# Moving the projections of three batches out of their own block and into the attention units

## The reference, cut to what matters

```python
x = x + tanh(g_ffn[0]) * L0_ffn(layernorm(x))          # experts; 4 result rows per token are summed
x = x + tanh(g_xattn[1]) * L1_xattn(layernorm(x), ctx)
# L1_xattn, 16 heads of 16: q = x @ Wq;  k, v = split(concat(ctx, x) @ Wkv)   (64 + 1024 keys)
# attn = softmax(causal(q @ k.T * 16**-0.5));  out = (attn @ v) @ Wout + bout
```

## Time and profile before

| what | value |
|---|---|
| runs | 1520.47, 1516.33, 1518.87 us; median 1518.87 us |
| the profiled execution | 1516.78 us, span 1514.7 us |
| busy over the span | PE 1098.5, DVE 1013.6, ACT 636.7, POOL 485.8 us |
| projection block | from 640.9 to 864.3 us of the span |
| attention block | from 864.3 to 1404.9 us |
| one unit in the steady part | 30.7 us |

### The profile page before, as it was taken

How to read it: one execution, slowest core, us unless ns; L and a number is a source line. 1 busy time by engine, 2 the same in 40 slices (tenths; PEclk the granted TensorE clock), 3 DMA queues, 4 the chain that set the end, 5 groups by cost and what they waited for, 6 DMA issues and landing times. The chain is left out here.

```text
span 1514.7 us, 23799 instructions
## 1 busy us (share of the span) xinstructions
PE 1098.5 (73%) x8155; PEld 563.8 (37%) x8155; DVE 1013.6 (67%) x1856; ACT 636.7 (42%) x1280; POOL 485.8 (32%) x539
## 2 busy tenths in 40 slices
PE   4799984342409999706556469999999999988757
PEld 2455553121206666403223213333333333331646
DVE  4989875454545666545554488888888888870675
ACT  1455653111103333202122117777777777775430
POOL 1334331767760000077886141111111111111110
PEclk8999997666659999957677759999999999996989
DMA  6010100222279999933676521111211121100003
GB/s 209 21 43 21 42 1 18 87 87 86 91 262 223 254 249 256 234 113 93 207 232 196 141 78 39 39 39 46 68 40 38 39 64 51 39 2 1 1 0 111
DMA packets 183649, 146.24 MB, mean 97 GB/s; under 512 B 102638, under 2 KB 160494, under 8 KB 183546
## 3 DMA queue, kind: packets, MB, share of 16 engines
q1 hardware_dynamic: 162570, 102.61, 25.8%
q0 software_dynamic: 12288, 33.57, 6.8%
q10 hardware_dynamic: 8688, 8.66, 1.8%
HBM read 53.11 MB, written 68.55 MB: 80 GB/s over the span
## 5 line engine op out<-in xcount | busy, mean ns | idle before, releaser
L1783 DVE TENSOR_REDUCE small<-ps 128x2 f32<-128x960 f32 (+6 forms) x384 | 378.7, 1040 | 53.9 <-PE ps L1839 51.6
L1762 ACT ACTIVATE region<-ps 128x512 f32<-128x512 f32 (+5 forms) x768 | 343.1, 533 | 107.3 <-PE ps L1853 106.5
L1733 POOL TENSOR_SCALAR_AFFINE_SELECT region<-region 128x512 f32<-128x512 f32 (+2 forms) x160 | 87.3, 546 | 423.6 <-ACT region L1762 423.6
L1853 PE MATMUL ps<-region 50*128 50x512 f16 (+5 forms) x896 | 198.3, 331 | 29.0 <-ACT region L1762 25.3
L1929 PE MATMUL ps<-region 128*32 128x512 f32 (+5 forms) x1792 | 191.7, 501 | 2.5 <-POOL region L1733 1.9
L860 POOL DMA_INDIRECT expert_rows<-region,small x128 | 131.3, 1026 | 64.0 <-issue 35.9
L1201 PE MATMUL ps<-region 128*128 128x384 f16 x696 | 124.0, 329 | 37.6 <-DMA region<-expert_rows 37.3
L1839 PE MATMUL ps<-region 48*128 48x480 f16 (+6 forms) x896 | 139.6, 333 | 15.1 <-DVE small L1783 15.1
L1366 POOL DMA_INDIRECT region<-result_rows,home x128 | 132.8, 1037 | 38.0 <-issue 36.3
L1853 PEld LDWEIGHTS ps<-region 50*128 50x128 f16 (+1 forms) x896 | 54.3, 95 | 211.1 <-ACT region L1762 197.0
L475 POOL TENSOR_TENSOR region<-region,small 128x1024 f32<-128x1024 f32 x32 | 60.9, 1915 | 117.2 <-DVE small L586 117.2
(11 more groups left out here) (237 smaller groups left out, 1730.3 us busy)
## 6 DMA issues: line engine op xcount, KB each, us to landing
result_rows<-region SPq DMA_DIRECT2D x58, 384.0 KB, 4.1
region<-v_parts SPq DMA_DIRECT2D x16, 576.0 KB, 3.8
v_parts<-region SPq DMA_DIRECT2D x14, 576.0 KB, 8.9
region<-k_parts SPq DMA_DIRECT2D x96, 68.0 KB, 2.2
region<-q_parts SPq DMA_DIRECT2D x96, 64.0 KB, 2.1
k_parts<-region SPq DMA_DIRECT2D x16, 272.0 KB, 5.4
x_sb<-in_x ACTq DMA_DIRECT2D x8, 512.0 KB, 9.6
region<-in_w13T SPq DMA_DIRECT2D x16, 256.0 KB, 3.0
```

Source lines behind the costliest of these rows:

```text
L1733: nc.gpsimd.affine_select(out=t, in_=t, compare_op=ALU.is_ge, fill=0.0, base=r0, pattern=[[0, G], [1, w]], channel_multiplier=-1).then_inc ...
L1762: nc.scalar.activation(dst, src, ACT.Exp, scale=SCALE).then_inc(s_exp, 1)
L1783: nc.vector.tensor_reduce(nmp[:, qt, :, p0:p0 + np_, place], s_pair(n + first)[:, :, 0:np_ * nk] .rearrange("p e (h k) -> p e h k", h=np_) ...
L1853: ins = nc.tensor.matmul(o, k_of(rr, tbuf)[:, pair, kt * P:kt * P + rows], q_of(rr, tbuf)[:, pair, q0:q0 + nq], start=True, stop=True)
```

## The change

In the projection block only the two chunks of batch 0 are projected; chunk 2 is also fetched, summed and normalised there, and half of chunk 3 is fetched. Everything else of chunks 2 to 7 becomes further words in the order of the units: `G` a fetch on POOL, `C` two additions on DVE (eight `C` to a chunk), `B`, `A`, `W`, `R` and `M` the steps of the normalisation, `X` the transposes, `Q`, `K`, `V` the products, and `x`, `q`, `k` the remainders on DVE. A product now fills a whole pair of banks and is read by one ACT and one DVE instruction of twice the width. It takes one of the two pairs of the scores and holds it until its remainder is taken (for values: until ACT has moved them). Chunk c's queries and keys come near the end of one unit, its values early in the next; the last 64 keys of a batch (`K.2`) come with the values. An entry of `BESIDE` names a value product `PV` and, between slashes, what is put behind that word, behind the next `T`, and behind the next score.

Unit 0's parts are copied inside SBUF (`load_first`, 24 DMAs) instead of being stored and loaded, while the stores of batch 0 (now in quarters) go on behind them. SP stores batches 1 to 3 within the attention, and a unit's loads wait for its batch's stores. The bias addition moves to units 11 and 12. Loops of DVE, POOL and SP over units are written out.

```diff
-        qp = view(region0, "qp", [P, 2 * PARTS, KH, L], F16)
+        yg = view(region0, "yg", [P, 4, FETCH, TOPK, D], F32)
+        def load_first(sp, done):
+            for dst, parts, slots in ((q_of, qp, Q_SLOTS), (k_of, kp, K_SLOTS)):
+                ...   # 2 halves x 3 slots x 2 pairs
+                            sp.dma_start(dst(r, 0)[:, p, :], parts[at_:at_ + DH, part, 0, :]).then_inc(done, 16)
             @block.sync        # projection block
-                for b in range(B):
-                    ...
+                sp.wait_ge(s_dve, moved(turn[0, "k10"]))
+                store_parts(sp, 0, slice(0, KH), slice(0, CH), slice(0, CH), s_pfirst)
+                sp.wait_ge(s_dve, moved(turn[1, "k02"]))
+                load_first(sp, s_unit0)
+                store_parts(sp, 0, slice(0, 1), slice(CH, L), slice(CH, KEYS), s_pfirst)
+                sp.wait_ge(s_dve, moved(turn[1, "k12"]))
+                store_parts(sp, 0, slice(1, KH), slice(CH, L), slice(CH, KEYS), s_pstored)
             @block.vector      # projection block
-                for c in range(2 * B):
-                    ...
+                combine(0, 0) ... normalised(1)
+                x_low(1)
+                low(1)
+                combine(2, 0)
+                combine(2, 1)
+                statistics(2)
+                normalised(2)
+        BESIDE = {
+            0: ("9 / / X2.0 X2.1 / x2.0", "10 / / Q2.0 Q2.1 C3.0 C3.1 C3.2 K2.0 K2.1 q2.0 C3.3 / ",
+                "11 / / G4.0 G4.1 / k2.0", ...),
+            1: ("0 / / G4.6 / ", "1 / / G4.7 / ", "3 / / V2.0 V2.1 / C3.4 C3.5", "4 / / / v2.0 C3.6 C3.7",
+                "5 / / G4.8 G4.9 / B3.0", "6 / / A3.0 G4.10 G4.11 / W3.0 R3.0", "7 / / G4.12 G4.13 / M3.0",
+                "8 / / G4.14 G4.15 / M3.1", "9 / / X3.0 X3.1 / x3.0",
+                "10 / / Q3.0 Q3.1 C4.0 C4.1 C4.2 K3.0 K3.1 q3.0 C4.3 / ", "11 / / / k3.0"),
+            2: ("3 / / K3.2 V3.0 V3.1 C4.4 k3.2 V3.2 v3.0 / C4.5", "4 / / / v3.2 C4.6 C4.7", "5 / / G5.0 / ",
+                "6 / / G5.1 / B4.0", "7 / / A4.0 G5.2 / W4.0", "8 / / G5.3 / R4.0", "9 / / / G5.4",
+                "10 / / / M4.0 G5.5", "11 / / G5.6 / M4.1", "12 / / / G5.7", "13 / / / G5.8"),
+            ...   # 3, 5, 7, 9 like 0; 4, 8 and 6, 10 like 1 and 2; 11, 12: two x four bias additions (Y)
+        def take(key, hold_):
+            free = [(slot + 1 + i) % FREE for i in range(FREE) if not held[(slot + 1 + i) % FREE]]
             @block.sync        # attention block
+                def load(v):
+                    sp.wait_ge(s_pstored, (v // NG + 1) * P_STORES + 1)
+                    load_parts(sp, v, v % NBUF, s_load[v % NBUF])
+                    sp.wait_ge(s_vstored, (v // NG + 1) * V_STORES + 1)
+                    load_values(v, v % NBUF)
+                def store(b):
+                    sp.wait_ge(s_sread, moved_at["K", 2 * b + 1, 2][1])
+                    store_parts(sp, b, slice(0, KH), slice(0, L), slice(0, KEYS), s_pstored)
+                    sp.wait_ge(s_vread, moved_at["V", 2 * b + 1, 2][1])
+                    for g in range(NG):
+                        store_values(sp, b, g)
+                for u in range(UNITS - 1):
+                    if u + 2 < UNITS:
+                        sp.wait_ge(s_pv, u * len(steps) + 2)
+                        load(u + 2)
+                    maxima(u, (u + 1) % NBUF)
+                    if u in (1, 5, 9):
+                        store(u // NG + 1)
             @block.tensor      # attention block
+                def next_parts(kind, c, i):
+                    ...
+                    if i % 2 == 0:
+                        wait_free(key)
+                        pe.wait_ge(s_sread, moved_at["X", c, 0][1])
```

More of the change, by code:

```diff
@@ L1527, in _ @@
                         ins.then_inc(s_full, 1)
-                    for n in VALUES[h]:
+                    for n in VALUES[c]:
                         t0, nt = VT[n]
@@ L1735, in _, with diagonal @@
-                units(pool, body)
+                def diagonal(u, k):
+                    hf, kt, q0, nq, on_diag = steps[k]
+                    if not on_diag:
+                        return
+                    last = max(i for i, (kk, _) in enumerate(t_list) if kk == k)
+                    pool.wait_ge(s_exp, u * N_T + T_FREE + 2 * (last + 1))
+                    rows = min(P, KEYS - kt * P)
+                    r0 = q0 - (kt * P - CTX)
+                    w = min(nq, P - r0)
+                    t = pT[0:rows, k % 2, :, 0:w]
+                    nc.gpsimd.affine_select(out=t, in_=t, compare_op=ALU.is_ge, fill=0.0, base=r0,
+                                            pattern=[[0, G], [1, w]], channel_multiplier=-1).then_inc(s_diag, 1)
@@ L1737, in _ @@
+                for u in range(-1, UNITS):
+                    for kind, *i in plans[u]:
+                        if kind == "PV":
+                            diagonal(u, i[0])
+                        elif kind == "G":
+                            fetch(*i)
+                        elif kind == "R":
+                            ln_pool(nc.gpsimd, i[0] - FIRST_C, s_var, s_rstd)
+                        elif kind == "Y":
+                            add_bias(i[0])
             @block.scalar
@@ new lines, in transposed_scores @@
+                def transposed_scores(of, i):
+                    tbuf = of % NBUF
+                    k, h0 = t_list[i]
+                    nq = steps[k][3]
+                    if of == 0 and i == 0:
+                        pe.wait_ge(s_ones, NBUF * 2 * 16)
+                    if i == 0:
+                        pe.wait_ge(s_mrow, (of + 1) * 32)
+                    for half in range(2):
+                        pe.wait_ge(s_exp, of * N_T + 2 * i + half + 1)
+                        if half == 0 and nq > CH // 2:
+                            product(tbuf, i, h0)
+                    if nq > CH // 2:
+                        product(tbuf, i, h0 + 1)
+                    else:
+                        for h in range(G):
+                            product(tbuf, i, h)
```

810 lines of the change are left out of this document (492 added, 318 removed), and 15 rows, old and new, of the table BESIDE.

## The result

| | before | after |
|---|---|---|
| median, timed side by side | 1519.31 us | 1551.51 us |
| ratio, with its 95% interval | | 1.0228 (1.0191 to 1.0266) |
| profiled execution, its span | 1516.78, 1514.7 us | 1551.13, 1549.2 us |
| last row sums of unit 15 (end of the attention's DVE work) | 1403.53 us | 1435.61 us |

The changed kernel is 2.3% slower; 1524 was forecast and the range ended at 1550. The attention does start much earlier, and the units pay more than that back. The first view is the timeline of the hand-over from the projection block: the stores of values that ACT issues, SP's copies of unit 0's parts and its sixteen quarter stores (start, length, instruction). The last row is DVE's first maximum of unit 0.

The account below looks back on a forecast made before the run. POOL's fetch queue was taken to bound the projection block, DVE's maxima and PE's hand-over the attention. Start -134.5, units' words +119.0, load wait +21.1 gave +5.6: 1524 us on the median, range 1488 to 1550.

Parts of the forecast that it names:

- The start: Hand-over from projection to attention: the attention starts at about 729.8 instead of 864.3, saving 134.5 us (bounds 123 to 138).
- 24 copies at 0.46 (2.76 / 6) are 11.0: SP's queue before the attention: unit 0's copies take 11.0 us, 0.46 each, beside 7.7 for sixteen quarter stores.
- margin of 1.7: At the attention's start: 1.7 us added for the barrier and the values that ACT stores at the same time.
- Queries and keys: Units 0, 1, 3, 5, 7, 9: X, Q, K and remainders cost 9.6 us per site, 57.6 for six.
- Units 4 and 8: Values 5.9 us per unit and normalisation 2.4, plus POOL's delays; 17.8 for the two units.
- so I add 1 us each: Units 2, 6, 10: 1 us each for PE's granted clock of 0.50 after idling at N0.
- The load wait: Units 2, 6, 10: PE waits at N0 for the values' load, 4.5, 4.5 and 9.1; 21.1 us with the clock.
- Rival (3): The chain of stores and loads takes about 35 us; N0 waits 12.5, 12.5 and 17: 1548 us, chance 0.23.
- Rival (1): Loads come in time in units 2, 6, 10, so nothing waits at N0: -15.5, 1503 us, chance 0.27.
- Rival (2): In the units DVE alone counts and PE's products hide below its words: -42, 1477 us, chance 0.12.
- POOL and the bias: Fetches and power between selects cost 4.3 in unit 1, bias additions 1.25 in units 11 and 12; 10.1 in all.
- Wrong "at its root": Signs against the forecast: no wait at N0, units 0 and 3 below 38 us, or an attention starting after 740.

Follow-up runs that it names:

- the three edits: Changed kernel with each batch's first unit stored first (batches 1 to 3), batch 0's quarter stores behind the barrier, POOL's fetches and powers behind the selects: 1514.33 us, 0.9966 of before.

## Why the prediction was wrong

The mechanism was right in the main: a saving at the attention's start, paid back in the units and in a wait for loads. Two terms failed: the price of the copies and stores at the start, and the lower clock behind the value products, which the sum left at nothing. The sum was short by 28.7 us on the profiled frame (34.35 for 5.6). Term by term:

| term of the sum | forecast | measured |
|---|---|---|
| attention's start | -134.5 | -119.7 |
| unit 0 | 9.6 | 11.8 |
| units 3, 5, 7, 9 | 39.3 | 38.1 |
| unit 1 | 23.2 | 24.3 |
| units 4 and 8 | 17.8 | 24.3 |
| units 2 and 6 with the load wait | 32.2 | 34.0 |
| unit 10 with the load wait | 15.5 | 14.9 |
| units 11 and 12 | 2.5 | 3.6 |
| units 13 to 15 | 0 | 1.0 |
| behind the attention | 0 | 2.4 |

(The forecast by units is the prediction's 119.0 + 21.1, laid out by the units that it names for each word. Behind the attention the work is the same; PE's mean granted clock there is 0.85 for 0.89, and no run looked further.)

**The start, 14.8 short.** The failing step is "24 copies at 0.46 (2.76 / 6) are 11.0". They took 20.8. The 0.46 was that of a load from DRAM, and of the cheaper of the two rows of loads in the earlier trace rows; a copy inside SBUF, which no row showed, takes 0.63 without the values' stores beside it and 0.87 with them. The 0.60 that I named as a bound is the mean of the two rows, and was near the 0.63; but for the likely value I took the lower row of another kind of transfer, and I gave the values that ACT stores only a share in a margin of 1.7. The 16 stores took 10.2 for 7.7 (0.63 each for 0.48). I had halved the price of a whole store; they have a quarter of its bytes (64 and 72 KB for 256 and 272) and still took two thirds of its time. The copies also began at 712.8 and not at 709.4, 3.4 later, and of the margin 1.0 was left over: 9.8 + 2.5 + 3.4 - 1.0 is the 14.8 but for rounding. The 3.4 I don't put to the change: POOL's first fetch of the block stands at 647.73 in the profile after, at 643.71 before, and between 641.9 and 647.1 in the experiments, which change nothing ahead of it.

**Queries and keys, right in size.** 9.6 per site was forecast; units 3, 5, 7 and 9 show 9.2 to 10.1. Unit 5 agrees part by part with the prediction's walk: the copy of `mT` comes 7.2 later (7.3 forecast), N0's maximum 0.7 more (0.6), the rest 1.4 more (1.7). The additions hide as it said. What it did not say is how little the products matter: with a third of them the chain shortens by 1.6, and the clock takes that back.

**Units 4 and 8, 6.5 short.** The failing step is the lower clock: the sum has it for the load wait alone ("so I add 1 us each") and leaves it at nothing behind the value products. Up to the maxima ahead of the last one the terms were right: in unit 4 DVE is through with them 7.9 us later than in the old unit, and the 5.9 for the values and 1.9 for the statistics come to 7.8. Then DVE waits for PE's last score and for `mT`:

```profile
1002.30 0.69 DVE L1965 TENSOR_REDUCE small<-ps 128x4 f32<-128x512 f32 x1 [2.34 <-PE ps L2090]
1006.46 0.68 DVE L1981 COPY small<-ps 8x1024 f16<-8x1024 f16 x1 [2.74 <-PE ps L2153]
```

In the earlier trace rows these waits are 0.20 and 1.28, so 3.6 us are added, where the sum has 0.6 for POOL; in unit 8, which has no fetches, they are 1.87 and 2.74. The value products leave PE busy 6.4 of 10 us, the clock stays at the lower level for 13.5 us behind them, and both waits lie in that spell; 0.8 of the 3.6 goes back to PE's wait for the late select. With the power behind the select, PE's wait for POOL was gone; these units came out at 39.3 to 39.9 in three kernels and at 42.5 in the fourth. So POOL is not shown to be the cause of the spell. Of the stretches shown, the shorter unit had the shorter spell; but in the kernel with the values behind the barrier unit 4 took 39.8 at a mean clock of 0.83, so where the spell lies counts as well, and what sets it is open.

**The load wait, right.** Taken at 4.5, 4.5 and 9.1, it was 4.5, 4.8 and 7.6, and taking it away gave 17.6 in the three units. The chain was 27.7 us in unit 2 (893.7, `k` taken and the first store issued, to 921.4), for the 27 taken. Rival (3), with 1548 the nearest in time, named a chain of 35, so its time was met by other causes. Rival (1) did not occur. Rival (2) did not occur either: DVE's busy time over the whole span hardly changed (1012.4 us for 1013.6), but PE and DVE wait for each other. The rule quoted there (the Trainium skill, "Perfetto Trace Analysis", Optimization Strategy), that interleaving regimes with different most-contended engines may improve performance, came true here only with the three edits, and then by 0.3%.

**POOL and the bias.** The 4.3 of unit 1 was about right: with its fetches out the unit fell by 4.0, and of two kernels with the same granted clock of 0.88 there, with and without, it took 54.7 and 51.6. The four bias additions of a unit cost 1.8 for 1.25. For a select beside DVE's additions I had added nothing: the changed kernel has a select of 0.80 us at 990.39 beside additions that run to 990.70. By the Trainium skill ("SBUF — State Buffer", Who interferes with whom) the two contend; the trace agrees: the six selects of this size that run beside such additions in the attention take 0.80 to 0.83 us, the 87 others that the timeline lists singly 0.62 to 0.65. That is 1 us in all, so leaving it out did little harm.

**The range** ended 1.5 us too low. Its lower part was drawn for rivals in which something goes better; the upper end stood on one mechanism, a longer chain, and not on SP's queue at its own bounds (123 instead of 134.5 saved, which alone moves the forecast to 1535) together with the units at theirs. Wrong "at its root" was to be seen by an attention that starts after 740, and that is what the trace shows: 744.6.

## What to carry to other kernels

When work moves between stages, what it costs there can be the chain of hand-overs over the buffer that it holds rather than its engine time, as it was here for queries and keys, though not for the values: walk one site through, and look for what is queued behind it. Ask also what the clock does behind a stretch in which the engine stands still part of the time. Store first what the next consumer loads, and put what nobody waits for behind the barrier and out from between the instructions that somebody does wait for; here that turned 2.3% slower into 0.3% faster with the same work. Price a transfer from a row of its own kind, or carry the whole gap between the bounds into the range.

## What the runs showed of the hardware

- Transfers of 32 and 34 KB inside SBUF cost the issuing queue 0.63 us each with the DMA engines busy 0.38 of the time, and 0.87 where they were busy 0.89 for a part of it. Stores of 64 and 72 KB cost it 0.63 each with the DMA engines busy 0.42, stores of 256 and 272 KB 0.97 with them busy 0.83.
- PE's granted clock fell to 0.50 behind stretches in which PE was busy 6.4 to 7.0 of 10 us, and was at that level for 7 to 13.5 us, although PE was then busy nine tenths of the time. The same unit 4 took 39.5 or 42.5 us in kernels that give it the same instructions (the three edits, and these with the bias additions moved).
- Unit 15, with the same instructions, took 37.54 us at a mean granted clock of 0.59 in the changed kernel (36.58 before) and 30.44 at 0.89 in the kernel with the values behind the barrier. So 7 us of difference between two profiles can lie in the clock of one unit:

```profile
1398.07:1435.61 37.54, 33.00 (x172) 6.55 (x169) 1.05 (x2) 20.37 (x46) 5.46 (x10) 0.59 0.00 1
```

```profile
1362.23:1392.67 30.44, 24.16 (x172) 6.28 (x170) 1.05 (x2) 20.37 (x46) 5.46 (x10) 0.89 0.01 1
```
